# Projection groups of the next batch in pairs at two places of a chunk's turn

## The chip, the core and the metric

The kernel runs on one core of one Trainium2 chip. Times are device microseconds of that core. Engines: PE (TensorE, matmuls; PEld is its weight load), DVE (VectorE), ACT (ScalarE), POOL (GpSimd), SP (SyncE, which issues the large transfers). Each has its own instruction queue, and they wait for each other by semaphores. PSUM has eight banks of 512 float32 a partition, into which PE writes and from which ACT and DVE read.

## The reference

The result is x plus attention of the layer-normed x plus a linear layer of it. x is 8 batches of 1024 rows of 256, all float32.

```
xn = _layernorm(x)
q, k, v = xn @ wq.T + bq, xn @ wk.T + bk, xn @ wv.T + bv
attn = softmax(einsum('bqd,bkd->bqk', q, k) * scale)
lilora_weight = up_aux @ (lora_up @ (lora_down @ down_aux))
out = x + einsum('bqk,bkd->bqd', attn, v) + xn @ W.T + b + xn @ lilora_weight.T
```

## The kernel before

All products are made in three parts from operands split in two: `hi` is the value rounded to PE's fp32r format, `lo` the rest, and a product is hi x hi, lo x hi and hi x lo (`split_products`, lines 748 to 753). PE therefore makes every large product of this kernel three times.

Scores need only one projection. With A = wq.T wk (made once), z = A applied to xn, and the scores of a key and a query are z times xn plus a term e of the key alone. The last linear layer is folded into the projection of v: the weights `vf` are 512 columns, of which 256 give v and 256 the linear layer's share, which goes straight to `base` (the output before attention is added).

**Groups.** A batch's projections are 16 groups, k = 0 to 15 (`group`, line 755). k 0 to 3 transpose xn (four 128x128 transposes each, line 768) and give xt; 4 to 7 make z (6 matmuls of 512 columns); 8 to 15 make v and the linear layer for one tile of 128 rows (6 matmuls of 512 columns). A group of batches 1 to 7 uses one of two PSUM banks, `g_ps[k % 2]`. It is emptied in two steps: ACT writes the hi part (`make_group_hi`, line 419), then DVE subtracts it from the bank to write the lo part (`make_group_lo`, line 548), and for a v group also adds the other 256 columns to base. Group k waits until DVE is done with group k - 2 (line 760).

**Chunks.** A batch has four chunks of 256 queries, numbered over all batches as g = 0 to 31. For a chunk PE makes four blocks of scores, `scores(g, j)`, each of two key tiles in bank `s_ps[j]`, and two blocks `p_times_v(g, u)`, each 24 matmuls for 128 queries into `o_ps[u]`. Between them: DVE takes a running maximum over the eight key tiles (`make_tile_max`, 2 instructions for each j), then the maximum over the partitions (`make_top`, 10 instructions), then subtracts it (`shift`, 4 instructions, which also empty s_ps); ACT takes the exponential in place (`make_p`, 2 for each j) and its hi part (`make_p_hi`); POOL the lo part (`make_p_lo`, two halves). `make_out` on DVE divides by the sum and adds to base; SP stores it. POOL also makes prod (for e), x plus bias, and the layer norm's factors; ACT normalises x (`make_xn`) and sums prod (`make_e_sum`).

**Order.** It is written by hand, the same for 29 turns (g = 0 to 28). In turn g PE makes the scores of chunk g + 1, then p times v of chunk g. The groups of the next batch are spread over this turn: PLACES = 4 groups in each of a batch's four chunks c, numbers 4c to 4c + 3, so chunk 0 has the transposes, chunk 1 z, chunks 2 and 3 v. The last batch has no groups. A prologue makes batch 0's own groups in one go, and the last chunks are a tail written out separately. No scheduler changes any of it.

Of the kernel before, what the change touches and what calls it, by code (L numbers as in the profile page):

```python
# [5 lines left out]
def attention_plus_lora_ffn(  # L6
# [35 lines left out]
    CHUNKS = S // Q  # L42
    KEYS = BANK // Q
    SB = TILES // KEYS
# [12 lines left out]
    NG = 2 * NT + TILES  # L57
# [14 lines left out]
    with ctx:  # L72
# [190 lines left out]
        PLACES = NG // CHUNKS  # L263
# [136 lines left out]
        def _(act):  # L400
# [18 lines left out]
            def make_group_hi(b, k):  # L419
                act.wait_ge(group_mm, NG * b + k + 1)  # L420
                ps = group_bank(b, k)
                if k < NT:
                    h, d = HALVES[k]
                    nc.scalar.activation(xt_hi[b % 2][:, d, half(h)], ps[:, :], ACT.Copy).then_inc(group_hi_made, 1)
                elif k < 2 * NT:
                    h, d = HALVES[k - NT]
                    nc.scalar.activation(zt_hi[b % 2][:, d, half(h)], ps[:, :], ACT.Identity,
                                         bias=z_bias[:, d:d + 1]).then_inc(group_hi_made, 1)
                else:
                    n = k - 2 * NT  # L430
                    nc.scalar.activation(v_hi[b % 2][:, n, 0:D], ps[:, 0:D], ACT.Copy).then_inc(group_hi_made, 1)  # L431
# [59 lines left out]
            for b in range(B):  # L491
                more = b + 1 < B
                for c in range(CHUNKS):
                    g = CHUNKS * b + c
                    if more:
                        if c > 0:
                            make_group_hi(b + 1, PLACES * c - 1)
                        make_group_hi(b + 1, PLACES * c)
                    if more and c == 2:
                        make_e_sum(b + 1, range(TILES // 2))  # L500
                    if b + 2 < B and c == 3:
                        make_xn(b + 2, range(TILES // 2))
                    if more:
                        make_group_hi(b + 1, PLACES * c + 1)
                    if more and c == 2:
                        make_e_sum(b + 1, range(TILES // 2, TILES))
                        make_e(b + 1)
                    if b + 2 < B and c == 3:
                        make_xn(b + 2, range(TILES // 2, TILES))
                    if g + 2 == CHUNKS * B:  # L510
                        for j in range(SB):
                            make_p(g + 1, j)
                            make_p_hi(g + 1, j)
                    elif g + 1 < CHUNKS * B:
                        make_p(g + 1, 0)
                        make_p(g + 1, 1)
                        make_p_hi(g + 1, 0)
                    if more:
                        make_group_hi(b + 1, PLACES * c + 2)
                    if g + 2 < CHUNKS * B:  # L520
                        make_p_hi(g + 1, 1)
                        make_p(g + 1, 2)
                        make_p(g + 1, 3)
                        make_p_hi(g + 1, 2)
                        make_p_hi(g + 1, 3)
                if more:
                    make_group_hi(b + 1, NG - 1)

        @block.vector
        def _(dve):  # L530
# [17 lines left out]
            def make_group_lo(b, k):  # L548
                dve.wait_ge(group_hi_made, NG * b + k + 1)
                ps = group_bank(b, k)  # L550
                if k < NT:
                    h, d = HALVES[k]
                    nc.vector.tensor_tensor(xt_lo[b % 2][:, d, half(h)], ps[:, :],
                                            xt_hi[b % 2][:, d, half(h)].bitcast(f32), ALU.subtract)\
                      .then_inc(group_done, 1)
                elif k < 2 * NT:
                    h, d = HALVES[k - NT]
                    nc.vector.scalar_tensor_tensor(zt_lo[b % 2][:, d, half(h)], ps[:, :], z_bias[:, d:d + 1],  # L558
                                                   zt_hi[b % 2][:, d, half(h)].bitcast(f32), ALU.add, ALU.subtract)\
                      .then_inc(group_done, 1)  # L560
                else:
                    n = k - 2 * NT
                    nc.vector.tensor_tensor(v_lo[b % 2][:, n, :], ps[:, 0:D], v_hi[b % 2][:, n, 0:D].bitcast(f32),  # L563
                                            ALU.subtract).then_inc(v_lo_made, 1)
                    if n == 0:
                        dve.wait_ge(x_bias_made, b + 1)
                    nc.vector.tensor_tensor(base[b % 2][:, n, :], ps[:, D:2 * D], base[b % 2][:, n, :], ALU.add)\
                      .then_inc(group_done, 1)
# [123 lines left out]
            for g in range(LAST - 2):  # L692
                b, c = divmod(g, CHUNKS)
                more = b + 1 < B
                if g > 0:
                    make_out((g - 1) // CHUNKS, (g - 1) % CHUNKS * QT + 1)
                if g > 0 and (g - 1) // CHUNKS + 1 < B:
                    make_group_lo((g - 1) // CHUNKS + 1, PLACES * ((g - 1) % CHUNKS) + 3)
                make_tile_max(g + 1, 0)
                make_tile_max(g + 1, 1)  # L700
                if more:
                    make_group_lo(b + 1, PLACES * c)
                make_tile_max(g + 1, 2)
                make_tile_max(g + 1, 3)
                make_top(g + 1)
                if more:
                    make_group_lo(b + 1, PLACES * c + 1)
                for j in range(SB):
                    shift(g + 1, j)
                make_out(b, c * QT)  # L710
                if b + 2 < B and c < 3:
                    if c == 0:
                        dve.wait_ge(x_loaded[b % 2], DMA * ((b + 3) // 2))
                    make_stats(b + 2, [range(0, 2), range(2, 5), range(5, TILES)][c])
                if b + 2 < B and c == 2:
                    make_mean_var(b + 2)
                if more:
                    make_group_lo(b + 1, PLACES * c + 2)


            make_out(B - 1, TILES - 3 * QT - 1)
# [25 lines left out]
        def _(pe):  # L747
# [151 lines left out]
            for g in range(LAST - 2):  # L899
                b, c = divmod(g, CHUNKS)  # L900
                more = b + 1 < B
                for j in range(SB):
                    scores(g + 1, j)
                    if more and j % 2 == 1:
                        group(b + 1, PLACES * c + j // 2)
                for u in range(QT):
                    p_times_v(g, u)
                    if more:
                        group(b + 1, PLACES * c + 2 + u)

            for j in range(SB):
                scores(LAST - 1, j)
# [32 lines left out]
```

## Time and profile before

| what | us |
|---|---|
| median of 3 runs | 545.03 |
| the 3 runs | 546.81, 545.02, 545.03 |
| the profiled execution | 545.94 |
| its span, first to last instruction | 544.1 |
| busy in the span: PE | 531.1 |
| DVE | 431.4 |
| ACT | 294.3 |
| POOL | 246.2 |
| mean granted TensorE clock, of full speed | 0.997 |

The profiled execution has 1.84 us outside its span. PE's matmuls are pipelined: a row's length is longer than the distance to the next row's start, and it is this distance that a stream of them costs. The loop of 29 turns lasts from 46.92 us to about 509 us of the span.

### The profile page before, as it was taken

To read this page: it belongs to the slowest core of one execution; us is meant where nothing else is said; L and a number is where in the kernel's file an instruction comes from. 1 tells how busy PE (TensorE), PEld (TensorE's weight loads), DVE (VectorE), ACT (ScalarE), POOL (GpSimd) and SP (SyncE) were. 2 spreads that over 40 slices of the span, in tenths; PEclk is the share of its full clock that TensorE was granted. 3 is DMA by queue.
4 is the path that set the end of the run, shared out by engine and by line. 5 is a ranking of instruction groups with operands and counts; after the bars stand their busy time and mean duration, and the time that the engine had idled before them with its cause. 6 is when DMAs were issued, how large, how long until landed. Compare 5 with 4: busy or idle time off the path is not lost.

```text
span 544.1 us, 10207 instructions
## 1 busy us (share of the span) xinstructions
PE 531.1 (98%) x3830; PEld 501.6 (92%) x3830; DVE 431.4 (79%) x1169; ACT 294.3 (54%) x717; POOL 246.2 (45%) x151
## 2 busy tenths in 40 slices
PE   5999999999999999999999999999999999999996
PEld 4788999999999999999999999999999999999995
DVE  3768789877887877877978778987788787777894
ACT  2656556535667337565356555653566733644344
POOL 3713852376333563545525755137634256333330
PEclk9989999999999999999999999999999999999999
DMA  8020011000200003000020002100000000000001
GB/s 245 19 78 1 20 34 64 20 21 22 96 20 20 2 20 97 21 20 20 1 97 20 21 20 61 37 20 21 20 20 21 21 1 20 20 21 20 20 3 56
DMA packets 9301, 18.90 MB, mean 35 GB/s; under 512 B 2240, under 2 KB 3876, under 8 KB 8356
## 3 DMA queue, kind: packets, MB, share of 16 engines
q1 hardware_dynamic: 7712, 18.09, 9.7%
q8 instruction: 30, 0.49, 0.4%
q10 hardware_dynamic: 1540, 0.16, 0.2%
q14 instruction: 19, 0.16, 0.1%
HBM read 9.86 MB, written 8.39 MB: 34 GB/s over the span
## 4 chain that ended last, share of the span: by engine, by line
PE 94%; DVE 3%; ACTq 1%; ACT 1%; issue 0%; POOL 0%; POOLq 0%
PE s_ps L750 11%; PE s_ps L752 11%; PE s_ps L751 11%; PE o_ps L822 11%; PE o_ps L826 11%; PE o_ps L824 11%; PE g_ps L750 8%; PE g_ps L751 8%; PE g_ps L752 8%; PE g_ps L768 2%; DVE stats L540 0%; ACTq L408 0%; DVE s L617 0%; PE o_ps L889 0%; PE o_ps L887 0%
## 5 line engine op out<-in xcount | busy, mean ns | idle before, releaser
L369 POOL TENSOR_TENSOR p_lo<-s,p_hi 128x1024 fp32r<-128x1024 f32 x62 | 149.2, 2408 | 266.7 <-ACT p_hi L456 257.3
L448 ACT ACTIVATE s<-s,e 128x256 f32<-128x256 f32 x256 | 109.5, 498 | 108.5 <-DVE s L617 108.4
L822 PE MATMUL o_ps<-v_hi,p_hi 128*128 128x258 f32 x512 | 146.2, 286 | 2.3 <-DVE base L635 2.2
L826 PE MATMUL o_ps<-v_hi,p_lo 128*128 128x258 f32 x512 | 144.5, 282 | 0.0
L750 PE MATMUL s_ps<-xt_hi,zt_hi 128*128 128x256 f32 x504 | 144.3, 286 | 0.0
L824 PE MATMUL o_ps<-v_lo,p_hi 128*128 128x256 f32 x512 | 144.1, 281 | 0.0
L752 PE MATMUL s_ps<-xt_hi,zt_lo 128*128 128x256 f32 x504 | 143.2, 284 | 0.0
L751 PE MATMUL s_ps<-xt_lo,zt_hi 128*128 128x256 f32 x504 | 143.0, 284 | 0.0
L583 DVE SCALAR_TENSOR_TENSOR tile_max<-s_ps,e,tile_max 128x256 f32<-128x256 f32 x221 | 106.9, 484 | 20.2 <-PE s_ps L752 10.3
L822 PEld LDWEIGHTS o_ps<-v_hi,p_hi 128*128 128x128 f32 x512 | 96.4, 188 | 4.6 <-DVE base L635 2.7
L824 PEld LDWEIGHTS o_ps<-v_lo,p_hi 128*128 128x128 f32 x512 | 97.2, 190 | 1.9
L750 PEld LDWEIGHTS s_ps<-xt_hi,zt_hi 128*128 128x128 f32 x504 | 96.5, 192 | 2.3 <-DVE zt_lo L558 0.4
L751 PEld LDWEIGHTS s_ps<-xt_lo,zt_hi 128*128 128x128 f32 x504 | 96.6, 192 | 1.8
L752 PEld LDWEIGHTS s_ps<-xt_hi,zt_lo 128*128 128x128 f32 x504 | 96.6, 192 | 0.0
L826 PEld LDWEIGHTS o_ps<-v_hi,p_lo 128*128 128x128 f32 x512 | 96.6, 189 | 0.0
L617 DVE TENSOR_TENSOR s<-s_ps,top 128x512 f32<-128x512 f32 x126 | 78.1, 677 | 0.1
L456 ACT ACTIVATE p_hi<-s 128x512 fp32r<-128x512 f32 x128 | 75.8, 619 | 0.1
L751 PE MATMUL g_ps<-vf_lo,xt_hi 128*128 128x512 f32 x124 | 49.0, 395 | 0.0
L750 PE MATMUL g_ps<-vf_hi,xt_hi 128*128 128x512 f32 x124 | 49.0, 395 | 0.0
L752 PE MATMUL g_ps<-vf_hi,xt_lo 128*128 128x512 f32 x124 | 49.0, 395 | 0.0
L431 ACT ACTIVATE v_hi<-g_ps 128x256 fp32r<-128x256 f32 x62 | 23.2, 374 | 47.0 <-PE g_ps L752 46.7
L563 DVE TENSOR_TENSOR v_lo<-g_ps,v_hi 128x256 fp32r<-128x256 f32 x62 | 25.5, 411 | 23.1 <-ACT v_hi L431 22.6
(122 smaller groups left out, 725.4 us busy)
## 6 DMA issues: line engine op xcount, KB each, us to landing
out<-base SPq DMA_DIRECT2D x31, 256.0 KB, 2.5
x_sb<-in_L_attn_x SPq DMA_DIRECT2D x7, 1024.0 KB, 5.8
x_sb<-in_L_attn_x SPq DMA_DIRECT2D x4, 256.0 KB, 6.5
s<-in_L_attn_wk SPq DMA_DIRECT2D x1, 256.0 KB, 3.0
s<-in_L_attn_wq SPq DMA_DIRECT2D x1, 256.0 KB, 6.4
s<-in_L_attn_wv SPq DMA_DIRECT2D x1, 256.0 KB, 6.5
s<-in_L_ffn_W SPq DMA_DIRECT2D x1, 256.0 KB, 6.9
out<-base SPq DMA_DIRECT2D x2, 128.0 KB, 1.9
```

Of the source, the lines that this page charges most:

```text
L369: nc.gpsimd.tensor_tensor(p_lo[g % 2][:, keys, :], s[:, keys, :], p_hi[g % 2][:, keys, :].bitcast(f32), ALU.subtract)\
L448: nc.scalar.activation(s[:, n, :], s[:, n, :], ACT.Exp, bias=e[b % 2][:, n:n + 1])\
L456: nc.scalar.activation(p_hi[g % 2][:, keys, :], s[:, keys, :], ACT.Copy).then_inc(p_hi_made, 1)
L563: nc.vector.tensor_tensor(v_lo[b % 2][:, n, :], ps[:, 0:D], v_hi[b % 2][:, n, 0:D].bitcast(f32), ALU.subtract).then_inc(v_lo_made, 1)
L583: nc.vector.scalar_tensor_tensor(tile_max[:, :], scores, e[b % 2][:, n:n + 1], tile_max[:, :], ALU.add, ALU.max).then_inc(tile_max_made, 1)
L617: nc.vector.tensor_tensor(s[:, KEYS * j:KEYS * (j + 1), :], score_bank(g, j)[:, :].rearrange("p (k q) -> p k q", k=KEYS), top[:, :].unsque ...
L750: nc.tensor.matmul(ps, left_hi(d), right_hi(d), start=(d == 0), stop=False)
L751: nc.tensor.matmul(ps, left_hi(d), right_lo(d), start=False, stop=False)
L752: mm = nc.tensor.matmul(ps, left_lo(d), right_hi(d), start=False, stop=(d == DT - 1))
L822: nc.tensor.matmul(o_ps[u][:, 0:D + ONES], p_hi[g % 2][:, n, q], v_hi[i][:, n, :], start=(n == 0), stop=False)
L824: nc.tensor.matmul(o_ps[u][:, 0:D], p_hi[g % 2][:, n, q], v_lo[i][:, n, :], start=False, stop=False)
L826: mm = nc.tensor.matmul(o_ps[u][:, 0:D + ONES], p_lo[g % 2][:, n, q], v_hi[i][:, n, :], start=False, stop=(n == TILES - 1))
```

## The change

Before, the four groups of a turn stand apart on PE: after the second and the fourth block of scores, and after each block of p times v. After, two follow the fourth block of scores, and two follow the second block of p times v. Their evictions move with them:

- on ACT, the hi parts of the last two groups of a turn both stand at the start of the next turn, behind all p_hi; before, the third stood between the first two p_hi of a turn;
- on DVE, the lo parts of these two stand together ahead of the maxima, and those of the first two stand together behind `make_top`; before, the first stood between the second and third block of maxima, and the third behind the batch-norm statistics.

The number and the shapes of all instructions stay.

```diff
                     g = CHUNKS * b + c
-                    if more:
-                        if c > 0:
-                            make_group_hi(b + 1, PLACES * c - 1)
-                        make_group_hi(b + 1, PLACES * c)
+                    if more and c > 0:
+                        make_group_hi(b + 1, PLACES * c - 2)
+                        make_group_hi(b + 1, PLACES * c - 1)
...
                     if more:
+                        make_group_hi(b + 1, PLACES * c)
                         make_group_hi(b + 1, PLACES * c + 1)
...
-                    if more:
-                        make_group_hi(b + 1, PLACES * c + 2)
...
                 if more:
+                    make_group_hi(b + 1, NG - 2)
                     make_group_hi(b + 1, NG - 1)
...
                 if g > 0 and (g - 1) // CHUNKS + 1 < B:
+                    make_group_lo((g - 1) // CHUNKS + 1, PLACES * ((g - 1) % CHUNKS) + 2)
                     make_group_lo((g - 1) // CHUNKS + 1, PLACES * ((g - 1) % CHUNKS) + 3)
-                make_tile_max(g + 1, 0)
-                make_tile_max(g + 1, 1)
+                for j in range(SB):
+                    make_tile_max(g + 1, j)
+                make_top(g + 1)
                 if more:
                     make_group_lo(b + 1, PLACES * c)
-                make_tile_max(g + 1, 2)
-                make_tile_max(g + 1, 3)
-                make_top(g + 1)
-                if more:
                     make_group_lo(b + 1, PLACES * c + 1)
...
-                if more:
-                    make_group_lo(b + 1, PLACES * c + 2)
...
                 for j in range(SB):
                     scores(g + 1, j)
-                    if more and j % 2 == 1:
-                        group(b + 1, PLACES * c + j // 2)
+                if more:
+                    group(b + 1, PLACES * c)
+                    group(b + 1, PLACES * c + 1)
                 for u in range(QT):
                     p_times_v(g, u)
-                    if more:
-                        group(b + 1, PLACES * c + 2 + u)
+                if more:
+                    group(b + 1, PLACES * c + 2)
+                    group(b + 1, PLACES * c + 3)
```

DVE, from the end of chunk 0's turn to the maxima of chunk 1's turn, before:

```order
L540 BN_STATS stats<-x_sb 128x6 x2
L553 TENSOR_TENSOR xt_lo<-g_ps,xt_hi 128x512
L633 RECIPROCAL p_sum_inv<-o_ps 128x1
L635 SCALAR_TENSOR_TENSOR base<-o_ps,p_sum_inv,base 128x256
L553 TENSOR_TENSOR xt_lo<-g_ps,xt_hi 128x512
L579 TENSOR_SCALAR tile_max<-s_ps,e 128x256
L583 SCALAR_TENSOR_TENSOR tile_max<-s_ps,e,tile_max 128x256 x3
L558 SCALAR_TENSOR_TENSOR zt_lo<-g_ps,b_parts,zt_hi 128x512
L583 SCALAR_TENSOR_TENSOR tile_max<-s_ps,e,tile_max 128x256 x4
L590 STREAM_TRANSPOSE tile_max_t<-tile_max 128x256
```

The same place on DVE, after:

```order
L539 BN_STATS stats<-x_sb 128x6 x2
L632 RECIPROCAL p_sum_inv<-o_ps 128x1
L634 SCALAR_TENSOR_TENSOR base<-o_ps,p_sum_inv,base 128x256
L552 TENSOR_TENSOR xt_lo<-g_ps,xt_hi 128x512 x2
L578 TENSOR_SCALAR tile_max<-s_ps,e 128x256
L582 SCALAR_TENSOR_TENSOR tile_max<-s_ps,e,tile_max 128x256 x7
L589 STREAM_TRANSPOSE tile_max_t<-tile_max 128x256
```

Both xt_lo now stand together ahead of the maxima, and the zt_lo among the maxima has moved behind the maximum over the partitions.

ACT, from the exponentials of chunk 0's turn to the first hi parts of chunk 1's turn, before:

```order
L448 ACTIVATE s<-s,e 128x256 x4
L456 ACTIVATE p_hi<-s 128x512
L424 ACTIVATE xt_hi<-g_ps 128x512
L456 ACTIVATE p_hi<-s 128x512
L448 ACTIVATE s<-s,e 128x256 x4
L456 ACTIVATE p_hi<-s 128x512 x2
L424 ACTIVATE xt_hi<-g_ps 128x512
L427 ACTIVATE zt_hi<-g_ps,b_parts 128x512 x2
```

The same place on ACT, after:

```order
L448 ACTIVATE s<-s,e 128x256 x4
L456 ACTIVATE p_hi<-s 128x512 x2
L448 ACTIVATE s<-s,e 128x256 x4
L456 ACTIVATE p_hi<-s 128x512 x2
L424 ACTIVATE xt_hi<-g_ps 128x512 x2
L427 ACTIVATE zt_hi<-g_ps,b_parts 128x512 x2
```

The xt_hi that stood between two p_hi now stands behind the fourth, beside the other.

## Rows read from the trace of the kernel before

**Rows 1.** The page's busy time, share of the span and instructions.
```profile
PE 531.1 (98%) x3830; PEld 501.6 (92%) x3830; DVE 431.4 (79%) x1169; ACT 294.3 (54%) x717; POOL 246.2 (45%) x151
```
**Rows 2.** Busy time by stretch: us, then busy us of each engine, clock, DMA.
```profile
243.16:307.63 64.47, 64.47 (x474) 61.28 (x473) 52.80 (x144) 36.23 (x89) 31.02 (x18) 1.00 0.10 34
```
**Rows 3.** Waits of PE over the span: us in total, times, longest.
```profile
PE s_ps L833 <- DVE base L533: 6.1, 1, 6.1
PE o_ps L822 <- DVE base L635: 2.2, 1, 2.2
```
**Rows 4.** Timeline of PE, chunk 0 of a batch: start us, length us, instruction.
```profile
240.11 0.28 PE L750 MATMUL s_ps<-xt_hi,zt_hi 128*128 128x256 f32 x1
...
242.99 0.60 PE L768 MATMUL g_ps<-identity,xn 128*128 128x128 f32 x4
...
243.55 0.28 PE L751 MATMUL s_ps<-xt_lo,zt_hi 128*128 128x256 f32 x1
```
**Rows 5.** Timeline of PE, end of chunk 1 of that batch.
```profile
266.19 0.28 PE L822 MATMUL o_ps<-v_hi,p_hi 128*128 128x258 f32 x1
...
269.06 0.40 PE L750 MATMUL g_ps<-xt_hi,a_hi 128*128 128x512 f32 x1
...
270.46 0.28 PE L750 MATMUL s_ps<-xt_hi,zt_hi 128*128 128x256 f32 x1
```
**Rows 6.** Timeline of PE, transposes of the prologue.
```profile
15.91 1.04 PE L768 MATMUL s_ps<-identity,xn 128*128 128x128 f32 x8
16.79 0.38 PE L864 MATMUL o_ps<-identity,base 128*128 128x128 f32 x2
```
**Rows 7.** Timeline of PE, the last two v groups of the prologue.
```profile
44.18 0.40 PE L750 MATMUL g_ps<-vf_hi,xt_hi 128*128 128x512 f32 x1
...
45.56 0.39 PE L750 MATMUL g_ps<-vf_hi,xt_hi 128*128 128x512 f32 x1
...
46.92 0.28 PE L750 MATMUL s_ps<-xt_hi,zt_hi 128*128 128x256 f32 x1
```
**Rows 8.** Timeline of DVE over that batch; in brackets the idle time before.
```profile
246.51 1.00 DVE L583 SCALAR_TENSOR_TENSOR tile_max<-s_ps,e,tile_max 128x256 f32<-128x256 f32 x2 [0.44 <-PE s_ps L752]
...
250.26 0.65 DVE L553 TENSOR_TENSOR xt_lo<-g_ps,xt_hi 128x512 fp32r<-128x512 f32 x1
250.84 2.47 DVE L617 TENSOR_TENSOR s<-s_ps,top 128x512 f32<-128x512 f32 x4
...
257.93 0.69 DVE L553 TENSOR_TENSOR xt_lo<-g_ps,xt_hi 128x512 fp32r<-128x512 f32 x1 [2.18 <-ACT xt_hi L424]
258.54 0.48 DVE L579 TENSOR_SCALAR tile_max<-s_ps,e 128x256 f32<-128x256 f32 x1
...
266.06 0.71 DVE L558 SCALAR_TENSOR_TENSOR zt_lo<-g_ps,b_parts,zt_hi 128x512 fp32r<-128x512 f32 x1
266.69 2.47 DVE L617 TENSOR_TENSOR s<-s_ps,top 128x512 f32<-128x512 f32 x4
...
305.91 0.42 DVE L563 TENSOR_TENSOR v_lo<-g_ps,v_hi 128x256 fp32r<-128x256 f32 x1 [1.83 <-ACT v_hi L431]
...
306.58 0.47 DVE L579 TENSOR_SCALAR tile_max<-s_ps,e 128x256 f32<-128x256 f32 x1
```
**Rows 9.** Timeline of ACT over that batch.
```profile
251.55 1.71 ACT L448 ACTIVATE s<-s,e 128x256 f32<-128x256 f32 x4 [4.00 <-DVE s L617]
...
253.68 0.57 ACT L424 ACTIVATE xt_hi<-g_ps 128x512 fp32r<-128x512 f32 x1
...
257.32 0.58 ACT L424 ACTIVATE xt_hi<-g_ps 128x512 fp32r<-128x512 f32 x1
...
305.52 0.36 ACT L431 ACTIVATE v_hi<-g_ps 128x256 fp32r<-128x256 f32 x1
```
**Rows 10.** Timeline of POOL, second half of a chunk's p_lo.
```profile
257.50 2.42 POOL L369 TENSOR_TENSOR p_lo<-s,p_hi 128x1024 fp32r<-128x1024 f32 x1 [0.16 <-ACT p_hi L456]
```
**Rows 11.** Busy time by stretch, a part of the prologue; columns as in rows 2.
```profile
34.00:36.00 2.00, 2.00 (x9) 1.71 (x8) 1.45 (x3) 2.00 (x5) 0.00 (x0) 0.52 0.00 0
```

## The prediction

> **What bounds the kernel now.** I read the page's busy shares first: PE is busy 98% of the span [rows 1]. A share says nothing about where the missing 2% lie, so the second view is the busy time in one batch's stretch, 243.16 to 307.63 us: PE is busy in all of its 64.47 us, DVE in 52.80, ACT in 36.23, at a granted clock of 1.00 [rows 2]. Third, the waits of PE: the two longest are 6.1 us for bq_col's copy at the very start and 2.2 us for the last chunks' base at the very end [rows 3]; neither lies in the loop that the change touches. So between about 47 and 500 us the time is the length of PE's own queue. The change can help only by making PE's instructions cheaper, and hurt only by making PE wait. It adds and removes no arithmetic.
>
> **PE's own cost, before.** Call S a block of scores (12 matmuls), P a block of p times v (24), T a transposing group (4 transposes), W a wide group (6 matmuls of 512 columns). Two S lie between 240.11 and 242.99 [rows 4]: S is 1.44 us. T and its neighbour's first matmul (0.12) lie between 242.99 and 243.55: T is 0.44. W runs from 269.06 to 270.46 [rows 5]: 1.40. P runs from 266.19 to 269.06: 2.87. So chunk 0 of this batch begins at 240.11, chunk 1 at 240.11 + 4 S + 4 T + 2 P = 253.37, chunk 2 at 270.46, and the next batch 64.47 after this one, at 304.58.
>
> **What pairing does to PE.** Two T in a row: in the prologue eight transposes and nothing else take from 15.91 to 16.79, 0.88 us [rows 6], exactly twice 0.44. The 14 pairs of T are costed at nothing. Two W in a row: in the prologue, where v groups follow each other, they last 44.18 to 45.56 and 45.56 to 46.92, so 1.38 and 1.36 us [rows 7], against 1.40 for a W between narrow matmuls. The bounds of a pair's gain are 0 (only where it stands changes) and 0.08 us (both groups at 1.36); no row shows a wide group above 1.40, so I set no loss. I take 0.02, since in a pair only the second group has a wide one ahead of it, and the nearest such row is the 1.38. Chunks 1 to 3 of seven batches hold 6 pairs each, 42 in all: 42 x 0.02 = 0.8 us, between 0 and 3.4.
>
> **What pairing does to the order elsewhere.** Two PSUM banks serve the groups, so group k may start when DVE has finished group k-2. I call a turn's four groups Ga, Gb, Gc, Gd. Now Gc and Gd end a turn together, and both evictions (hi on ACT, then lo on DVE) stand behind ACT's last p_hi of the turn. I follow one batch in the trace's own time, with the durations of before, to see whether a PE instruction comes to wait.
>
> Chunk 0: the fourth S ends at 240.11 + 5.76 = 245.87, 0.44 sooner than before, since no T is among them. DVE began its last two maxima 0.20 after that end and the next xt_lo 3.75 later (246.51 to 250.26) [rows 8]; now at 246.07 and 249.82. Two xt_lo of 0.58 to 0.61 stand there instead of one, so shift starts at 251.02, where it was 250.84. ACT's first exp follows 0.71 later [rows 8, 9]: 251.73, 0.18 late. From it to the end of the last p_hi, ACT took 5.77 (251.55 to 257.32) with one xt_hi inside, 0.57 long and overlapping its neighbour by some 0.1 [rows 9]. Without it 5.3 is left, so the hi of Gc starts at 257.03, its lo 0.61 later at 257.64 (as 257.32 to 257.93 before), and its bank is free 0.69 after that, at 258.33. PE wants this bank for Ga of chunk 1 at 253.37 + 5.76 = 259.13. **This is the tightest new wait, with 0.8 us to spare.** Gb wants the bank of Gd at 260.53, and that is free at 258.94.
>
> Chunk 1: maxima from 258.86 (were 258.54). Eight of them and top took 266.06 - 258.54 less one zt_lo of about 0.66, or 6.86 [rows 8]; then two zt_lo, 1.3. Shift starts at 267.02 (was 266.69), exp at 267.73. Ga's lo is done at 265.72 + 0.71 = 266.43, and Gc wants its bank at 270.46 - 2.80 = 267.66: 1.2 to spare. Chunk 2: hi of Gc at 267.73 + 5.3 = 273.03, its lo 0.7 later and done at 274.44, PE's Ga at 270.46 + 5.76 = 276.22: 1.8 to spare. Maxima from 275.03, top done at 281.89, two v_lo with base at 0.67 each (305.91 to 306.58 [rows 8]), exp at 283.94. Chunk 3: hi at 289.24, lo 0.39 later (305.52 to 305.91 [rows 8, 9]), maxima from 290.97, exp at 299.88. Next chunk 0: hi at 305.18, lo at 305.57, first maximum at 306.91, the last two at 306.91 + 6 x 0.52 = 310.03. PE's fourth S ends at 304.58 + 5.76 and is seen 0.20 later, at 310.54. So DVE waits for PE there, **with 0.5 us to spare in a batch**, and lateness does not pile up.
>
> POOL: the second half of p_lo started at 257.50 and ran 2.42 [rows 10]. It goes with the last p_hi, now about 0.3 sooner, and P's second half needs it no sooner than 253.37 + 5.76 + 2.80 + 1.44 = 263.37. ACT's sums of prod (chunk 2) and xn (chunk 3) stand between the same evictions as before, in a gap that ends with the exp. Stores and loads on SP follow out_made, which moves by tenths. Behind the last group (from about 500 us) the program is the same.
>
> Sum: the profiled execution of 545.94 us is 544.1 of span and 1.84 outside; minus 0.8 gives 543.3 and 545.1. On the median of 545.03 it is 544.2.
>
> **A rule of the Trainium skill against this.** The row first: PE has no bubble in the loop [rows 2]. The Trainium skill, Perfetto Trace Analysis, section Optimization Strategy, says that one gap repeating on an engine that should be saturated can mean that SBUF or PSUM had no room for the next tile. By that rule groups that take both banks at once would bring such a gap in each turn; by the walk above the banks are free 0.8 to 1.8 us ahead, and no gap comes. No run shown here decides it.
>
> **Rivals.** (1) The eviction loop takes over, and the kernel is slower. The loop is: last p_hi, hi of Gc, lo of Gc and Gd, eight maxima, top, two lo, shift, exp, p_hi. Before, only one lo stood between ACT's last p_hi and the maxima; now both do. The walk leaves it 0.5 us a batch, so it decides from an error of 0.13 us a chunk. At 0.3 us a chunk PE would wait 4 x 0.3 - 0.5 = 0.7 us a batch, 4.9 in all: 549.9. For it: DVE is busy 52.80 of 64.47 us, and a late instruction would hit it. Against it: all durations are of the same instructions in the same neighbourhood. (2) The wide pairs give all that the bound allows: 3.4 us, 541.6. Against it: the 1.36 appeared only after several wide groups in a row [rows 7]. (3) The clock falls. It granted 1.00 in the loop [rows 2] and 0.52 for 2 us in the prologue [rows 11]; 1.9 us at the lower of the two levels (1.2 GHz against 2.4) cost about 1 us. Once in every pair of T that would be 14 us, 558. Against it: PE stays busy, and only the 0.88 us of T is new.
>
> **Numbers.** The forecast with what lies inside 0.5% (2.7 us, about what a measurement of this kernel can tell from no change): 0.85. Rival 1 beyond 0.5%: 0.10. Rival 3: 0.01. Rival 2 beyond 0.5%: 0.04. That makes slower 0.11. The range: below, about half of the pairs' bound, 542.8; above, rival 1 at some 0.22 us a chunk, (4 x 0.22 - 0.5) x 7 = 2.7, so 547.8.
>
> **What would show it.** PE busy for the whole of each batch's stretch, 64.2 to 64.5 us; no wait of PE on xt_lo, zt_lo or base in the loop; two W in 2.76 to 2.80; two T in 0.88; DVE waiting for the fourth S in chunk 0 of each batch; ACT's first exp 0.1 to 0.4 later in its turn than before. It would be wrong if PE waits in front of the first group of a batch's second turn, or if the batch's stretch grows while DVE no longer waits for S.

## The result

| | us | runs |
|---|---|---|
| kernel before | 545.11 | 6 |
| changed kernel | 549.18 (547.75 to 549.95) | 6 |
| ratio | 1.0061, 95% interval 1.0046 to 1.0077 | |

The change makes the kernel slower by 0.6% by this ratio; the medians are 4.1 us apart. The forecast was 544.2 and the range ended at 547.8, so the measured time lies above the range. What happened is the first rival, the eviction loop, which had a chance of 0.10.

A second set on another chip, with ten runs of the changed kernel and 21 of the one before, gave 1.0043 (1.0027 to 1.0060). Part of the difference between the sets is the clock. In some executions of either kernel PE runs at the lower clock level for a stretch of 3.4 us in the prologue, in the tail, or in both, and the mean granted clock of a run tells roughly how many (1.00 for none, 0.997 for one, 0.994 for two). In the second set, spans at a mean clock of 1.00 are 543.0 on the mean before (5 runs) and 545.4 changed (3 runs); at 0.997 they are 544.7 (10) and 546.9 (6). So the change itself costs 2.2 to 2.4 us. The remaining 1.7 us of the first comparison is not seen in these equal-clock pairs, and no run ties it to the change. Added to the median before, 2.2 to 2.4 us give 547.3 to 547.5, just inside the range of the forecast: the direction was wrong in any case, but what carried the time beyond 547.8 is, as far as the two sets show, the lower clock: five of the six runs of the changed kernel have one such stretch or two.

### The profile page after: what moved, and what is told of

Read it like the earlier page. It is cut to its first block, busy times and chain, and to the rows that moved or that the text cites. A ratio compares the mean times of both kernels' runs of the same rounds, so it can differ in the third digit from the quotient of the medians.

```text
span 548.2 us, 10207 instructions
## 1 busy us (share of the span) xinstructions
PE 533.4 (97%) x3830; PEld 503.5 (92%) x3830; DVE 430.3 (78%) x1169; ACT 293.0 (53%) x717; POOL 246.0 (45%) x151
## 4 chain that ended last, share of the span: by engine, by line
PE 50%; DVE 27%; ACT 16%; issue 4%; DMA 1%; SPq 0%; POOL 0%; DVEq 0%; POOLq 0%
DVE tile_max L582 9%; ACT s L448 9%; ACT p_hi L456 6%; PE o_ps L817 6%; PE o_ps L821 6%; PE o_ps L819 6%; PE s_ps L745 6%; PE s_ps L747 6%; PE s_ps L746 6%; PE g_ps L745 5%; PE g_ps L746 5%; PE g_ps L747 5%; DVE xt_lo L552 3%; DVE s L616 2%; DVE base L566 2%
## 5 line engine op out<-in xcount | busy, mean ns | idle before, releaser
L456 ACT ACTIVATE p_hi<-s 128x512 fp32r<-128x512 f32 x128 | 72.9, 616 | 0.1
L416 ACT ACTIVATE xn<-x_sb,shift_rstd,rstd 128x256 f32<-128x256 f32 x60 | 31.0, 591 | 28.2 <-POOL shift_rstd L341 28.2
```

The source lines that it names most:

```text
L416: nc.scalar.activation(xn[:, n, :], x_sb[b % 2][:, n, :], ACT.Identity, bias=shift_rstd[:, n:n + 1], scale=rstd[:, n:n + 1]).then_inc(xn_m ...
L456: nc.scalar.activation(p_hi[g % 2][:, keys, :], s[:, keys, :], ACT.Copy).then_inc(p_hi_made, 1)
```

## The profile after

The page of the changed kernel begins like that of before [rows 1]: PE 97% busy now, DVE no busier than it was.

```profile
PE 533.4 (97%) x3830; PEld 503.5 (92%) x3830; DVE 430.3 (78%) x1169; ACT 293.0 (53%) x717; POOL 246.0 (45%) x151
```

The view of busy time by stretch, over the same 64.47 us as in [rows 2], shows PE 0.13 us short of full, and over the tail a granted clock of 0.95 (columns: us, busy us of PE, PEld, DVE, ACT, POOL, then clock and DMA):

```profile
243.16:307.63 64.47, 64.34 (x474) 61.14 (x473) 52.69 (x144) 35.88 (x90) 30.93 (x17) 1.00 0.10 34
511.00:548.20 37.20, 31.61 (x246) 30.85 (x244) 26.72 (x68) 16.63 (x36) 9.62 (x4) 0.95 0.08 29
```

The waits of PE, changed kernel (us in total, times, longest). The first two were there before [rows 3]. Of the four waits of the third, one lies in the prologue, where the kernel before had one too; the other three, 1.2 us, are new and lie in the loop:

```profile
PE s_ps L828 <- DVE base L532: 6.7, 1, 6.7
PE o_ps L817 <- DVE base L634: 2.4, 2, 2.2
PE g_ps L745 <- DVE xt_lo L552: 1.8, 4, 0.6
```

PE's timeline of the changed kernel shows where it is, at the first group of chunk 1 (start us, length us, instruction; in brackets the idle time before), in two batches:

```profile
194.68 0.28 PE L747 MATMUL s_ps<-xt_hi,zt_lo 128*128 128x256 f32 x1
195.57 0.50 PE L745 MATMUL g_ps<-xt_hi,a_hi 128*128 128x512 f32 x1 [0.61 <-DVE xt_lo L552]
...
259.85 0.28 PE L747 MATMUL s_ps<-xt_hi,zt_lo 128*128 128x256 f32 x1
260.26 0.50 PE L745 MATMUL g_ps<-xt_hi,a_hi 128*128 128x512 f32 x1
```

A start 0.12 us after its neighbour would be PE at work; here it is 0.89 and 0.41, so PE stood still for 0.77 and 0.29. The second carries no bracket, since the neighbour's modelled end covers most of the gap. The list of waits therefore undercounts these, and the distance between starts is the better measure. By it, turn 1 of the seven batches takes 17.09, 17.30, 18.00, 17.46, 17.50, 17.48 and 17.82 us, while turns 2 and 3 take 16.99 to 17.01 in every batch. Without a wait turn 1 takes 17.09 or 17.07 (the kernels with a shorter circle, below), so the waits in it are 0, 0.2, 0.9, 0.4, 0.4, 0.4 and 0.7 us (the restart included: the first wide matmul behind a wait starts 0.34 ahead of the next, not 0.23).

The first score matmuls of the loop, of a batch in its middle, of the next batch, and of the last batch start at:

```profile
46.93 0.28 PE L745 MATMUL s_ps<-xt_hi,zt_hi 128*128 128x256 f32 x1
...
240.97 0.28 PE L745 MATMUL s_ps<-xt_hi,zt_hi 128*128 128x256 f32 x1
...
305.59 0.28 PE L745 MATMUL s_ps<-xt_hi,zt_hi 128*128 128x256 f32 x1
...
499.97 0.28 PE L745 MATMUL s_ps<-xt_hi,zt_hi 128*128 128x256 f32 x1
```

The seven batches take 453.04 us. In the kernel before the loop starts at 46.92 [rows 7] and the last batch here:

```profile
497.78 0.28 PE L750 MATMUL s_ps<-xt_hi,zt_hi 128*128 128x256 f32 x1
```

That makes 450.86. The loop has lost 2.2 us. The batch in the middle takes 64.62, where 64.47 stood. The rest of this execution's 4.1 us is in the tail, mostly the lower clock there.

DVE, chunk 0 to chunk 1 of the batch that corresponds to [rows 8]:

```profile
244.66 0.47 DVE L578 TENSOR_SCALAR tile_max<-s_ps,e 128x256 f32<-128x256 f32 x1
245.17 3.81 DVE L582 SCALAR_TENSOR_TENSOR tile_max<-s_ps,e,tile_max 128x256 f32<-128x256 f32 x7
249.09 0.45 DVE L589 STREAM_TRANSPOSE tile_max_t<-tile_max 128x256 f32<-128x256 f32 x1
...
259.51 1.29 DVE L552 TENSOR_TENSOR xt_lo<-g_ps,xt_hi 128x512 fp32r<-128x512 f32 x2 [2.31 <-ACT xt_hi L424]
260.72 0.47 DVE L578 TENSOR_SCALAR tile_max<-s_ps,e 128x256 f32<-128x256 f32 x1
...
265.15 0.45 DVE L589 STREAM_TRANSPOSE tile_max_t<-tile_max 128x256 f32<-128x256 f32 x1
```

In chunk 0 all seven later maxima run in one row with no wait for PE; before, the last two waited 0.44 us for the fourth block of scores. DVE is not brought into step by a wait for PE any more. The eight maxima take 265.15 - 260.72 = 4.43 us.

ACT shows the period of the circle, from the first exp of chunk 0 to that of the next batch:

```profile
253.61 1.71 ACT L448 ACTIVATE s<-s,e 128x256 f32<-128x256 f32 x4 [5.16 <-DVE s L616]
...
269.79 1.71 ACT L448 ACTIVATE s<-s,e 128x256 f32<-128x256 f32 x4 [5.78 <-DVE s L616]
...
318.26 0.91 ACT L448 ACTIVATE s<-s,e 128x256 f32<-128x256 f32 x2 [5.19 <-DVE s L616]
```

That is 64.65 us, longer than the 64.47 that PE needed for a batch before. The period alone would not tell which engine sets it, since all engines of the loop come to share one. What tells is that in this stretch DVE waits for ACT and ACT for DVE, neither waits for PE on that circle, and PE waits for DVE at its first z group.

## Experiments

**Theories.** L: the eviction loop sets the time, and it is longer than I had worked out by 0.2 us a turn, because eight maxima in a row cost more than the same eight with another instruction between them. D, its mechanism: each maximum must wait for the end of the one ahead of it. Rivals: B, only the two banks held by a pair matter; C, the clock; N, a pair itself costs PE time.

**The changed kernel again** (no edit).

> The changed kernel again, beside the others on one chip. Theory L (the eviction loop): last p_hi, hi and lo of the turn's last two groups, eight maxima, top, two lo, shift, exp make a circle of 64.7 us a batch, longer than PE's 64.4, so PE waits for the first group of chunk 1: batches of 64.6 to 65.3 us as before, 2 to 2.4 us lost by 500 us of the span. Theory C (clock): a second 3.4 us stretch at the half clock appears behind 530 us and costs 1.7; it is the change's doing only if it appears in most executions of this kernel and in few of the kernel before. Both together: 549.2; if the clock's part is chance, 547.5.

548.66 us, ratio 1.0043 (1.0027 to 1.0060). From the first score matmul of the loop to that of the last batch 452.98 us: 2.1 us lost again, where the first profile has 2.2. Its profile has a mean clock of 1.00, no lower stretch, and a span of 545.9. Five of the 21 runs of before and three of the ten of this have that clock, 10 and 6 have 0.997. So the lower stretch comes with either kernel, and the loss in the loop comes without it. C does not explain the loss.

**A useless instruction in the changed kernel, and the same in the kernel before.**

```diff
+                nc.vector.reciprocal(spare[:, 32 * (g % 2):32 * (g % 2) + 32], bias_all[:, 0:32]).then_inc(spare_made, 1)
                 for j in range(SB):
                     make_tile_max(g + 1, j)
```

> The changed kernel with one short instruction of no use on DVE (a reciprocal of 32 columns, some 0.2 us) in each turn ahead of the maxima. Theory L: DVE and ACT's circle sets the batch, so each turn is 0.2 longer one for one: 28 x 0.2 = 5.6 us more than the changed kernel, about 555. Rival B (PE is the bound but for a few waits for a bank): the wait at chunk 1 grows by what the lateness adds there, some 0.4 a batch, 3 us more. Theory C (clock alone): no change.

> The kernel before with the same short instruction at the same place. Theory L: the circle has about 1.5 us a batch to spare and 4 x 0.2 fits in: 545.1 within 1. If DVE's work bounded the kernel before as well, 5.6 us more, 550.7.

In the changed kernel: 552.23 us, ratio 1.0119 (1.0094 to 1.0145), 3.6 us over the changed kernel on the same chip. In the kernel before: 546.36, ratio 1.0002 (0.9988 to 1.0016). The sizes need the DVE timeline of the first of the two:

```profile
261.54 0.34 DVE L701 RECIPROCAL spare<-bias_all 128x32 f32<-128x32 f32 x1
261.80 0.38 DVE L580 TENSOR_SCALAR tile_max<-s_ps,e 128x256 f32<-128x256 f32 x1
```

The instruction puts the maxima 0.26 us back, and they then take 4.34 instead of 4.43, so a turn grows by 0.17 and a batch by 0.69. The fourth to the sixth batch grow from 64.61 to 64.71 us to 65.31 to 65.35, by 0.64 to 0.70: one for one. The total is less than my 5.6, since the first batch has room (64.29 in both), since 0.17 is not 0.2, and since the third and the seventh batch, which late instructions of DVE (below) had made longer already, grow by only 0.1 and 0.4. The time alone, 3.6 us, stands nearer to B's 3 than to L's 5.6; the one-for-one growth of the undisturbed batches is what speaks for L. The kernel before, whose batches stay at 64.35 and 64.48, has room for the same 0.17 a turn, at no cost.

**The maxima in a row, in the kernel before.**

```diff
                 make_tile_max(g + 1, 1)
-                if more:
-                    make_group_lo(b + 1, PLACES * c)
                 make_tile_max(g + 1, 2)
                 make_tile_max(g + 1, 3)
                 make_top(g + 1)
                 if more:
+                    make_group_lo(b + 1, PLACES * c)
                     make_group_lo(b + 1, PLACES * c + 1)
```

> The kernel before with one move on DVE alone: the lo of a turn's first group no longer stands between the maxima but behind top, so the eight maxima follow each other in a row. Theory L: a maximum waits for the one ahead of it, and the lo between them hid one such wait; in a row they take 4.43 us where 4.23 was left after taking off the lo. The loop is then 63.7 us a batch, still under 64.4, and the time stays: 545.1 within 1. Rival B (only the two banks matter, the row of maxima costs nothing): 4.23 and 545.1 too. So the time tells nothing, the stretch from the first maximum to the transpose in chunk 1 does: 4.43 or 4.23.

570.95 us, ratio 1.0449 (1.0425 to 1.0472): far off my expectation. Where DVE does not wait for PE the maxima took 4.42 us, as L says, but I had forgotten the bank. Here PE asks for the third group right behind the first P of the turn, and the lo of the first group, now behind top, is not done by then. PE's waits of this kernel:

```profile
PE g_ps L767 <- DVE xt_lo L553: 8.3, 7, 1.2
...
PE g_ps L749 <- DVE zt_lo L558: 4.8, 7, 1.0
PE g_ps L749 <- DVE base L567: 4.5, 14, 0.7
```

That is one wait in each of the 28 turns. The changed kernel avoids it only because its third group comes behind both P, 2.87 us later.

**One half of the change at a time.** First pair alone: Ga and Gb behind the scores, Gc and Gd placed and evicted as before. Second pair alone: the reverse. In both, ACT and DVE follow; the cuts show PE's part.

```diff
                 for u in range(QT):
                     p_times_v(g, u)
-                if more:
-                    group(b + 1, PLACES * c + 2)
-                    group(b + 1, PLACES * c + 3)
+                    if more:
+                        group(b + 1, PLACES * c + 2 + u)
```

> One part of the change alone: the turn's first two groups in a pair behind the scores, the last two apart and evicted as in the kernel before. Theory L: only the row of maxima is added to the circle, 0.2 a turn, and with 63.7 us a batch it stays under PE's 64.4: no wait of PE in the loop, 545.1, less at most 0.7 for the 21 pairs. Rival N (a pair itself costs PE time): half of the change's loss, 547.

```diff
                 for j in range(SB):
                     scores(g + 1, j)
-                if more:
-                    group(b + 1, PLACES * c)
-                    group(b + 1, PLACES * c + 1)
+                    if more and j % 2 == 1:
+                        group(b + 1, PLACES * c + j // 2)
```

> The other part alone: the turn's last two groups in a pair, evicted together ahead of the maxima, the first two apart, the first of them wanted behind the second block of scores. Both theories see the bank: PE asks for the last turn's third group's bank at 1.44 x 2 = 2.9 us into the turn, and its lo is done at some 4.9 (chunk 1), 4.0 (chunk 2) and 2.8 (chunk 3): about 2 + 1.1 us a batch, 7 batches, so 20 us more, 565. Theory L adds nothing to that, since PE's own waits then open the circle. If the bank's wait costs nothing: 545.1.

First pair alone 559.24, ratio 1.0235 (1.0213 to 1.0258); second pair alone 566.02, ratio 1.0359 (1.0337 to 1.0381). Waits of PE, first of the one, then of the other:

```profile
PE g_ps L764 <- DVE xt_lo L552: 5.2, 7, 0.8
PE g_ps L746 <- DVE zt_lo L557: 4.9, 7, 1.0
```

```profile
PE g_ps L749 <- DVE xt_lo L553: 12.9, 8, 1.8
```

The first missed by what I had missed above: with the first evictions behind top, the third group asks too early, 0.8 to 1.0 us in chunks 0 and 1. The second behaved as expected in chunk 1 (turns of 19.1 to 19.2 us in three of the seven batches), but chunks 2 and 3 stayed at 17.0: with PE held up in chunk 1, the lo of the third group in chunk 2 is done 2.1 us into PE's turn, where I had expected 4.0 and PE asks at 2.9. In the other four batches that turn took 20.7, which is the clock (last section). In the loop the halves cost 13 and 20 us by themselves and 2.2 together. Each needs the other: a group asks for the bank of the next but one ahead of it, and with wide groups that distance on PE, from start to start, is 8.5 us for all four groups before, and 8.5 or 8.6 with the full change, but only 5.7 for one of the four with either half: for the third group with the first pair alone, for the first with the second.

**Shortening the circle, PE's order unchanged.** Two maxima ahead of the lo parts:

```diff
+                make_tile_max(g + 1, 0)
                 if g > 0 and (g - 1) // CHUNKS + 1 < B:
                     make_group_lo((g - 1) // CHUNKS + 1, PLACES * ((g - 1) % CHUNKS) + 2)
                     make_group_lo((g - 1) // CHUNKS + 1, PLACES * ((g - 1) % CHUNKS) + 3)
-                for j in range(SB):
+                for j in range(1, SB):
                     make_tile_max(g + 1, j)
```

> The changed kernel with the first two of the eight maxima ahead of the lo parts of the last two groups, in the time in which DVE waits for ACT. Theory L: that takes 1.1 us a turn out of the circle; it falls to about 60.5 us a batch, PE is the bound again, no wait of PE in the loop, 544.2 to 545.1. Rival B (the pair's hold of both banks is what costs): the lo parts are done no sooner than in the changed kernel, so the waits at chunk 1 stay, 547.5. Theory C: unchanged, 549.2.

And only the fourth group's lo put behind the first two maxima:

```diff
                     make_group_lo((g - 1) // CHUNKS + 1, PLACES * ((g - 1) % CHUNKS) + 2)
+                make_tile_max(g + 1, 0)
+                if lo:
                     make_group_lo((g - 1) // CHUNKS + 1, PLACES * ((g - 1) % CHUNKS) + 3)
-                for j in range(SB):
+                for j in range(1, SB):
                     make_tile_max(g + 1, j)
```

> The changed kernel with only one instruction group moved: the lo of the turn's fourth group stands behind the first two maxima, not ahead of them. The same work is in the circle, but the lo now hides one wait between two maxima, 0.2 a turn. Theory L with the row of maxima as the step that failed: the circle is 0.8 us a batch shorter than 64.7, PE sets the time, few waits of PE, 544.5 to 545.5. If the order among the maxima is of no matter: 547.5 to 549.2.

544.66 us, ratio 0.9977 (0.9964 to 0.9991), and 545.28 us, ratio 0.9978 (0.9966 to 0.9990). Both have batches of 64.29 and 64.23 us and no wait of PE in the loop. The first fence below is the kernel with two early maxima, its first score matmul of the loop and that of the last batch; the one behind it is the other kernel, chunk 1:

```profile
45.84 0.28 PE L746 MATMUL s_ps<-xt_hi,zt_hi 128*128 128x256 f32 x1
...
495.71 0.28 PE L746 MATMUL s_ps<-xt_hi,zt_hi 128*128 128x256 f32 x1
```

```profile
256.60 0.48 DVE L578 TENSOR_SCALAR tile_max<-s_ps,e 128x256 f32<-128x256 f32 x1
257.11 0.48 DVE L582 SCALAR_TENSOR_TENSOR tile_max<-s_ps,e,tile_max 128x256 f32<-128x256 f32 x1
257.51 0.68 DVE L552 TENSOR_TENSOR xt_lo<-g_ps,xt_hi 128x512 fp32r<-128x512 f32 x1
258.11 3.21 DVE L582 SCALAR_TENSOR_TENSOR tile_max<-s_ps,e,tile_max 128x256 f32<-128x256 f32 x6
261.43 0.45 DVE L589 STREAM_TRANSPOSE tile_max_t<-tile_max 128x256 f32<-128x256 f32 x1
```

From the first maximum to the transpose 4.83, of which the xt_lo takes 0.60: 4.23 for the eight. The xt_lo starts 0.40 after the maximum ahead of it, where a maximum would have started 0.51 to 0.55 after it. So this kernel has the changed kernel's work in the circle less 0.20 a turn, and that alone removes the waits. B falls too: PE's placing of the pairs is untouched, and the waits that B had stay at chunk 1 are gone in both kernels. From 45.84 to 495.71 the kernel with early maxima takes 449.87 us, 1.0 less than the kernel before. That is the pairs' own gain, and N falls with it.

**Taking away the wait from one maximum to the next.** Two running maxima, one for even and one for odd key tiles, in the changed kernel, joined by one more instruction; and the same with early maxima.

```diff
...
-                        dve.wait_ge(tile_max_made, TILES * g + n)
+                        dve.wait_ge(tile_max_made, TILES * g + n - 1)
...
+                nc.vector.tensor_tensor(tile_max[:, :], tile_max[:, :], tile_max_b[:, :], ALU.max).then_inc(joined, 1)
+                dve.wait_ge(joined, g + 1)
                 nc.vector.transpose(tile_max_t[:, :], tile_max[:, :]).then_inc(max_t_made, 1)
```

> The changed kernel with two running maxima, one for even and one for odd key tiles, joined by one more instruction ahead of the transpose: no maximum waits for the one directly ahead of it. PE, ACT and the placing of the pairs are those of the changed kernel. Theory D (each maximum waits for the end of the one ahead, that is what the row costs): starts fall from 0.55 us apart to some 0.40, as independent instructions of DVE overlap by 0.08; eight of them and the join take 3.8 us, not 4.43; the circle is 2.4 us a batch shorter, no wait of PE in the loop, 543.7 to 545. If a maximum costs 0.55 by itself: 4.43 + 0.5 and a circle 2 us a batch longer, 563.

> Two running maxima and the first two maxima ahead of the last groups' lo parts, together. In the loop PE is the bound with the early maxima alone already, so nothing is left to gain there. In the tail behind 510 us DVE's maxima lie on the chain that ends last: two chunks of them, 0.6 each at most. So 543.5 to 544.7, and 0 to 1.2 below the kernel with the early maxima alone.

554.25 us, ratio 1.0151 (1.0131 to 1.0171), and 557.41, ratio 1.0212 (1.0190 to 1.0235). Both slower, against D as it stood. DVE, first kernel, chunk 1, then chunk 2:

```profile
263.63 0.47 DVE L586 SCALAR_TENSOR_TENSOR tile_max<-s_ps,e,tile_max 128x256 f32<-128x256 f32 x1
264.03 0.47 DVE L586 SCALAR_TENSOR_TENSOR tile_max_b<-s_ps,e,tile_max_b 128x256 f32<-128x256 f32 x1
264.60 2.30 DVE L593 TENSOR_TENSOR tile_max<-tile_max,tile_max_b 128x256 f32<-128x256 f32 x1
266.94 0.45 DVE L595 STREAM_TRANSPOSE tile_max_t<-tile_max 128x256 f32<-128x256 f32 x1
...
282.22 0.42 DVE L593 TENSOR_TENSOR tile_max<-tile_max,tile_max_b 128x256 f32<-128x256 f32 x1
```

The maxima now start 0.40 apart, as D says. The join spoils it: 0.42 us in chunk 2, but 2.30 in chunk 1. The timeline of POOL shows what it does meanwhile:

```profile
262.00 4.62 POOL L350 TENSOR_TENSOR base<-x_sb,bias_all 128x2048 f32<-128x2048 f32 x1
```

It ends at 266.62, the join at 266.90; at the join of chunk 2 POOL is idle. The join is the one instruction of DVE in this loop with two SBUF tiles as inputs and no PSUM. In the second kernel, with early maxima as well, the join was as long as 3.09 us, and batches took 65.5 to 65.9. To part the join from the two maxima themselves, the next kernel joins them without such an instruction:

```diff
-                nc.vector.tensor_tensor(tile_max[:, :], tile_max[:, :], tile_max_b[:, :], ALU.max).then_inc(joined, 1)
+                nc.vector.transpose(two_max_t[:, 0, :], tile_max[:, :]).then_inc(joined, 1)
+                nc.vector.transpose(two_max_t[:, 1, :], tile_max_b[:, :]).then_inc(max_t_made, 1)
...
```

> The changed kernel with two running maxima again, but joined without an instruction that reads two SBUF tiles: each is transposed by itself, and the reduction after it runs over both. Theory D, with the join of the two-maxima kernel held up by POOL as what spoiled it there (that join took 2.30 us where POOL worked on base, 0.42 to 0.53 elsewhere): eight maxima at 0.39 and a second transpose, less 0.55 apart as before, take the circle down by some 0.5 us a turn, 2 us a batch; no wait of PE in the loop, batches of 64.3 us, 544.2 to 545.2. If two running maxima themselves lengthen the circle: batches of 65.2 as there, 552 to 554.

546.44 us, ratio 1.0005 (0.9992 to 1.0018), against 1.0043 and 1.0061 for the changed kernel. Batches of 64.29 and 64.23, no wait of PE in the loop, so the loop gains as much as with early maxima. Its time is over my 544.2 to 545.2. Its profile shows the same loop, 449.87 us, and a tail with a stretch at the lower clock: from the start of the last batch to the end it takes 48.1 us, the profile of the kernel with one lo between the maxima, which has such a stretch too, 47.8, and that with two early maxima, which has none, 46.3. So most of the excess is the clock, and why ten of its twelve runs have the stretch is open. DVE in chunk 1:

```profile
258.66 0.48 DVE L584 TENSOR_SCALAR tile_max<-s_ps,e 128x256 f32<-128x256 f32 x1
...
261.99 0.45 DVE L595 STREAM_TRANSPOSE two_max_t<-tile_max 128x256 f32<-128x256 f32 x1
...
262.86 0.69 DVE L599 TENSOR_REDUCE quad_max<-two_max_t 128x8 f32<-128x512 f32 x1
```

Eight maxima in 3.33 us instead of 4.43. The second transpose and the longer reduction take part of that back: from the first maximum to the end of top it is 6.63, against 7.07 in the changed kernel, and those 0.4 a turn are enough. D stands: the 0.55 was a wait for the one ahead, not work.

**The version that beats both, again.**

> The kernel with the first two maxima ahead of the lo parts of the last two groups once more, for the size of what it brings: the pairs' 1.0 us (batches of 64.26 on the mean against 64.42) and nothing else, so 0.998 of the kernel before, 0.9965 to 0.9995.

544.34 us, ratio 0.9982 (0.9967 to 0.9997). Two sets agree: pairs with two maxima ahead of the lo parts are 0.2% faster than the kernel before. At a mean clock of 1.00 its spans are 542.2 on the mean (6 runs in each set) against 542.9 to 543.1, so the change with this order is worth 0.7 to 0.9 us. The medians are further apart, 1.6 to 1.9 us, because more of its runs have a mean clock of 1.00: 12 of 22, against 13 of 44 of the kernel before. Whether that is chance was not tried.

## Why the prediction was wrong, point by point

**Right: PE was the bound, and there was only a wait to lose.** No other view was needed for that.

**Right: the cost on PE.** Eight transposes and the 0.12 us of the next matmul take from 52.68 to 53.68 in the first turn, so a pair of T is 0.88 us, as in [rows 6]. The pairs were costed at 0.8 us for 42; the loop of the kernels without waits is 1.0 us shorter, all of it in the turns with wide groups.

**Right: the place of the tightest wait**, Ga of chunk 1 behind the lo of the last turn's third group. Practically all new waits of the loop are there; the others come to under 0.2 us (0.1 in turn 0 of the third batch and in that of the last).

**Wrong: the eight maxima and top, sized at 6.86.** The step is "eight of them and top took 266.06 - 258.54 less one zt_lo of about 0.66". These are the rows that it goes by, from the kernel before:

```profile
258.54 0.48 DVE L579 TENSOR_SCALAR tile_max<-s_ps,e 128x256 f32<-128x256 f32 x1
259.05 1.59 DVE L583 SCALAR_TENSOR_TENSOR tile_max<-s_ps,e,tile_max 128x256 f32<-128x256 f32 x3
260.56 0.74 DVE L558 SCALAR_TENSOR_TENSOR zt_lo<-g_ps,b_parts,zt_hi 128x512 fp32r<-128x512 f32 x1
261.22 2.11 DVE L583 SCALAR_TENSOR_TENSOR tile_max<-s_ps,e,tile_max 128x256 f32<-128x256 f32 x4
263.43 0.45 DVE L590 STREAM_TRANSPOSE tile_max_t<-tile_max 128x256 f32<-128x256 f32 x1
```

It takes the inserted instruction off at its full spacing, 0.66, but a part of that time was the wait from the fourth maximum of the row to the fifth, which the zt_lo had filled. Without it the wait shows: 4.43 for eight maxima, not 4.23, so with the 2.63 of top 7.06, not 6.86. Turn by turn, from first exp to first exp, the circle was 0.15 to 0.19 longer than in the walk, 64.65 us a batch where the walk gave about 63.96. The walk's other steps held: 5.30 from exp to the hi of Gc (253.61 to 258.91), 0.60 to its lo, 2.63 for top.

**Wrong: the weight of the margin.** The text said that rival 1 decides from an error of 0.13 us a chunk, and still gave it 0.10, on the ground that all durations came from the same neighbourhood. The change's point is that the neighbourhood is another. The 0.5 was itself too large. The walk set the circle's 63.96 against PE's batch of before, 64.47, but the pairs' own gain shortens that to 64.26 on the mean, which leaves 0.3 a batch. With an error of 0.69 a batch PE then waits 0.39, and the fourth to the sixth batch show 0.40 to 0.42. Over the seven batches the waits are 3.2 us (453.04 less 449.87), and the pairs give 1.0 back. The sum of the text with 0.2 a chunk, (4 x 0.2 - 0.5) x 7 = 2.1, meets the measured 2.2 by luck: it leaves out that the first two batches have room left (waits of 0 and 0.2) and that the third and the seventh wait longer (1.0 and 0.7). Those two have to do with single late instructions of DVE. In the third batch of the changed kernel the maxima show one, a row of seven broken by 0.46 of idle time:

```profile
180.12 1.59 DVE L582 SCALAR_TENSOR_TENSOR tile_max<-s_ps,e,tile_max 128x256 f32<-128x256 f32 x3
182.17 2.11 DVE L582 SCALAR_TENSOR_TENSOR tile_max<-s_ps,e,tile_max 128x256 f32<-128x256 f32 x4 [0.46 <-DVE tile_max L582]
```

The maxima take 4.78 there instead of 4.43, and PE's longest turn, 18.00, follows at once. Four of the loop's 29 rows of maxima have such a gap, at the same places in both profiles of the changed kernel, and the kernel before has one too. Where there is no slack it goes on to PE: the last of the four stands ahead of the long wait of the seventh batch. What delays these instructions was not tried.

**Half right: the price of rival 1.** 4.9 us at 0.3 a chunk was the right mechanism at a larger error and a larger room; they were 0.17 and 0.3, and 549.9 came near the measured 549.18 only with the clock's help.

**The rule on PSUM room.** I set it aside because the walk found banks free 0.8 us ahead. The Trainium skill, Perfetto Trace Analysis, section Optimization Strategy, says that a repeated gap can mean missing SBUF or PSUM room. A repeated gap did come, and PE does wait for a bank, but more banks are not what it lacks in the first place: with the same two banks the kernels with a shorter circle have no gap.

## What to carry to other kernels

Take a loop of waits as a circle, add it up, and compare it with the bound engine's period; when less than a few per cent is left, the change is decided by terms of 0.1 us, and a slower outcome is not a side case. Count the change's own gain on the bound engine too, because it shortens the period and eats room. A duration got by taking an inserted instruction out of a row of dependent ones can be too short: here the inserted one was filling a wait. If a dependent row of short instructions lies on such a circle, put independent work between them, or ahead of the moment at which the engine waits anyway.

## What the runs showed of the hardware that I had not expected

**DVE's dependent instructions.** With a semaphore wait on the one ahead, maxima of 0.48 us start 0.55 apart; without it, 0.39 to 0.40. So a wait for the instruction directly ahead, on the same engine, cost 0.15 us each time. The edit took away the wait and the shared tile together; which of the two costs the time is not parted.

**DVE and POOL.** The join with two SBUF inputs took 0.42 us alone and 2.30 while POOL's addition ran, ending 0.28 behind it; its longest in the loop was 2.32 us, and 3.09 in the kernel that also has early maxima. With one SBUF input the maxima, transposes and reductions show nothing of the kind. The Trainium skill, SBUF — State Buffer, section Who interferes with whom, says that a DVE instruction with two SBUF inputs contends with a GpSimd instruction that reads SBUF, and that the one that issues first keeps the shared port for its whole length. The trace agrees: POOL's addition started first, at 262.00, and the join lasted until just behind its end.

**PE's clock after a wait.** In the second pair alone, PE waited about 1.8 us at chunk 1 of each batch. After the third to the sixth such wait the granted clock fell to the lower level for 3.4 us, after the first two and the last it did not. Busy time by stretch of that kernel, where its PE rows stand 0.43 apart instead of 0.23:

```profile
190.00:197.00 7.00, 5.20 (x45) 5.00 (x44) 4.62 (x12) 6.35 (x14) 3.62 (x2) 1.00 0.10 37
197.00:200.60 3.60, 3.60 (x12) 3.02 (x12) 2.39 (x6) 0.69 (x1) 3.60 (x2) 0.53 0.00 0
```

The four batches take 67.9 us instead of 66.4: a wait of 1.8 us cost 1.5 more in four of seven. What decides between them was not found. The waits of the changed kernel, up to 0.8 us, brought none of this inside the loop.
